# The gate product and the residual sum of each routed block, moved from VectorE to GpSimd

## The reference, cut to what matters

```
h = layernorm(x) * (1 + ca) + sa
x = x + ga * mixer(h)                        # the part that the change touches
h = layernorm(x) * (1 + cb) + sb
scores = softmax(h @ gate_w.T); the best 2 of 8 experts per token
x = x + gb * (sum over the 2 experts + silu(h @ sw1.T) * (h @ sw2.T) @ sw3.T)
```

## Time and profile before

| | us |
|---|---|
| median of 3 runs | 2100.26 |
| lowest and highest | 2099.86, 2103.84 |
| the profiled execution | 2101.66 |
| its span in the trace | 2099.8 |

### The profile page before, as it was taken

The page is one execution under the profiler, slowest core; times in us unless marked ns, Lnnn a source line. Parts: engine busy times, 40 slices in busy tenths (PEclk is TensorE's granted clock), DMA queues, the critical chain, the costliest instruction groups (busy, mean ns, idle before and its releaser), DMA issues.

```text
span 2099.8 us, 25086 instructions
## 1 busy us (share of the span) xinstructions
PE 1815.3 (86%) x6766; PEld 825.8 (39%) x6766; DVE 1938.2 (92%) x1839; ACT 1559.2 (74%) x3223; POOL 1791.2 (85%) x607
## 2 busy tenths in 40 slices
PE   7898898979797888889897979797877599999997
PEld 3323332323232323233332323242312156668996
DVE  7988999999999999999999999999999977746776
ACT  5886879797978888776779797979876444446664
POOL 5689999999999999999999999999999834324555
PEclk9989898989898988989898989898967699999999
DMA  7745454453535362635454453535361483224554
GB/s 264 241 122 139 117 136 112 112 131 108 129 105 130 95 160 67 157 90 138 109 137 113 118 127 110 127 109 121 85 150 43 148 326 118 89 101 81 95 97 74
DMA packets 140219, 264.24 MB, mean 126 GB/s; under 512 B 21376, under 2 KB 43904, under 8 KB 138928
## 3 DMA queue, kind: packets, MB, share of 16 engines
q1 hardware_dynamic: 125488, 240.90, 42.6%
q0 software_dynamic: 13296, 17.80, 4.9%
q10 hardware_dynamic: 1296, 3.93, 0.5%
HBM read 193.36 MB, written 70.26 MB: 126 GB/s over the span
## 4 chain that ended last, share of the span: by engine, by line
ACT 27%; DVE 25%; PE 24%; issue 15%; POOL 6%; DMA 1%; DVEq 0%; ACTq 0%; POOLq 0%; SPq 0%
DVE hst L1656 17%; ACT psum L1282 11%; DVE dbu L1635 6%; PE psum L2260 5%; POOL hst L963 4%; ACT dbu L1314 3%; PE psum L2347 3%; PE psum L2356 3%; PE psum L2367 3%; PE psum L2273 3%; PE psum L2102 2%; POOL dbu L951 2%; ACT L1211 2%; PE psum L2034 1%; ACT sp_tmp L1251 1%
## 5 line engine op out<-in xcount | busy, mean ns | idle before, releaser
L963 POOL TENSOR_TENSOR hst<-hst,c_rep 128x2048 f32<-128x2048 f32 x254 | 1145.0, 4534 | 5.8 <-DVE hst L1656 5.8
L1656 DVE TENSOR_TENSOR_SCAN hst<-psum,state,dbu 128x1024 f32<-128x1024 f32 x384 | 879.0, 2329 | 0.3 <-PE psum L2102 0.2
L1282 ACT ACTIVATE psum<-dt_rep,neg_a 128x512 f32<-128x512 f32 (+1 forms) x1024 | 660.2, 676 | 151.1 <-DVE hst L1656 148.5
L1635 DVE TENSOR_TENSOR dbu<-psum,b_rep 128x2048 f32<-128x2048 f32 x176 | 398.2, 2262 | 3.3 <-PE psum L2087 3.3
L951 POOL TENSOR_TENSOR dbu<-dtu_rep,b_rep 128x2048 f32<-128x2048 f32 x80 | 363.7, 4546 | 16.5 <-DVE hst L1656 11.5
L2102 PE MATMUL psum<-hst,same 128*32 128x512 f32 x2048 | 275.4, 686 | 53.6 <-POOL hst L963 47.4
L2087 PE MATMUL psum<-dt,same 32*128 32x512 f32 x352 | 217.0, 699 | 119.7 <-DVE dbu L1635 105.2
L1656 DVE TENSOR_TENSOR_SCAN hst<-psum,dbu 128x1024 f32<-128x1024 f32 x128 | 286.6, 2272 | 12.7 <-ACT psum L1282 8.8
L2034 PE MATMUL psum<-xp,taps 128*128 128x512 f32 x512 | 236.8, 606 | 9.5 <-ACT sp_tmp L1248 9.5
L1072 POOL DMA_INDIRECT out_x<-h,target_u x71 | 111.5, 1571 | 120.0 <-DVE h L1952 51.8
L2102 PEld LDWEIGHTS psum<-hst,same 128*32 128x32 f32 x2048 | 66.5, 124 | 271.1 <-issue 166.9
(11 more groups left out here) (194 smaller groups left out, 2566.8 us busy)
## 6 DMA issues: line engine op xcount, KB each, us to landing
dt_rep<-dt_scratch SPq DMA_DIRECT2D x256, 256.0 KB, 4.7
dtu_rep<-dtu_scratch SPq DMA_DIRECT2D x320, 64.0 KB, 1.9
taps<-taps_scratch SPq DMA_DIRECT2D x64, 256.0 KB, 4.4
b_rep<-bc_scratch SPq DMA_DIRECT2D x64, 256.0 KB, 5.1
c_rep<-bc_scratch SPq DMA_DIRECT2D x64, 256.0 KB, 7.7
dt_scratch<-dt SPq DMA_DIRECT2D x48, 256.0 KB, 6.1
h<-slot_scratch SPq DMA_DIRECT2D x71, 129.5 KB, 2.5
sp_tmp<-t_scratch SPq DMA_DIRECT2D x16, 512.0 KB, 6.9
```

What stands on the lines that cost most here:

```text
L963: nc.gpsimd.tensor_tensor(h, h, c_rep[q % 2][:], ALU.mult).then_inc(prod_done, 1)
L1282: nc.scalar.activation(psum[:, PS_A + i, kept], dt_rep[:, G % 2, j, kept], ACT.Exp, scale=neg_a[:, q % 2, u, i:i + 1]).then_inc(exp_done, 1)
L1635: nc.vector.tensor_tensor(dbu[:, U % DBU, :, :], psum[:, PS_U:PS_U + 1, :].broadcast_to((P, NG, TB)), b_rep[U // UNITS % 2][:], ALU.mult). ...
L1656: nc.vector.tensor_tensor_scan(both(hst[:, U % RING, groups, :]), both(psum[:, PS_A + 2 * pair:PS_A + 2 * pair + 2, :]), both(dbu[:, U % D ...
```

## The change

Both instructions of `add_mixed` move from VectorE to GpSimd, with the same operands. On GpSimd the blocks 0 and 1 come straight behind the last `weigh` and in front of the first two `norm_power`; block `p + 1` comes at the start of iteration `p`, in front of `scatter(p - 1, 0)`, and so straight behind `scatter(p - 2, 1)`. SyncE, ScalarE and TensorE keep their programs. The semaphore `f_x1` is now raised by GpSimd.

```diff
+            def add_mixed(p):
+                n, half = TAKEN[p], p % 2
+                pool.wait_ge(f_in[half], 32 * (p // 2) + 32)
+                block_x1 = x1[:, rows_of(n), :]
+                gates = fmod[:, n // SEG, 0:1, :].broadcast_to((P, NT, DM))
+                nc.gpsimd.tensor_tensor(tin[:, half], tin[:, half], gates, ALU.mult).then_inc(f_x1, 1)
+                pool.wait_ge(f_x1, 2 * p + 1)
+                nc.gpsimd.tensor_tensor(block_x1, block_x1, tin[:, half], ALU.add).then_inc(f_x1, 1)
...
+            pool.wait_ge(f_gate_loaded, 32)
+            for p in range(2):
+                add_mixed(p)
             for p in range(2):
                 norm_power(p)
...
             for p in range(NBLK):
+                if 0 < p < NBLK - 1:
+                    add_mixed(p + 1)
                 if p > 0:
                     scatter(p - 1, 0)
...
-            def add_mixed(p):
...
             dve.wait_ge(f_gate_loaded, 32)
-            add_mixed(0)
             norm_statistics(0)
...
-            add_mixed(1)
             norm_statistics(1)
...
             for p in range(1, NBLK - 1):
                 shared(0, p - 1)
-                add_mixed(p + 1)
                 shift_logits(p)
```

## The result

| | before | after |
|---|---|---|
| median | 2100.97 (4 runs, 2099.86 to 2103.84) | 2123.23 (4 runs, 2121.62 to 2128.80) |
| the profiled execution | 2101.66 | 2122.43 |
| its span | 2099.8 | 2120.5 |

The kernel before has one run more here than in the table ahead of the prediction. The change makes the kernel 1.06% slower: ratio 1.0106, 95% interval 1.0087 to 1.0126, or +22.3 us. The forecast was +8.3 us, and the range ended at 2114.5. The direction and both places of the loss were as forecast. The size was not.

The account below looks back on a forecast made before the run. TensorE was taken to bound the routing period, so freeing VectorE pays almost nothing. The terms 2.4 - 0.5 + 1.2 + 5.2 = +8.3 us gave a median of 2108.6 us, range 2101.5 to 2114.5.

Parts of the forecast that it names:

- block 2's sum gone from beside the first scatter DMA: First routing period: scatter(0, 0)'s first DMA shortens from 1.47 to 0.96 us, on the path, -0.5 us.
- GpSimd's two-input 128x1024: Length of each moved instruction on GpSimd, from a line through sizes 512 and 2048: 2.36 us.
- collision A: Mixer's end: GpSimd's block 0 product runs between VectorE's two last mixer products, delaying sum_chunk: +2.4 us (0 to +4.7).
- collision B: End of rank_experts: GpSimd's mixing holds short VectorE instructions, delaying behind: +1.2 us in the first period, +5.2 over four.
- other moves, SyncE's loads, the power: Routing stage: SyncE's loads, scatter(p - 1, 0) and norm_power have time in hand, no cost.
- What bounds the kernel: Routing stage: TensorE is busy the whole 23.0 us period, VectorE has over 5 us idle.
- The port: SBUF port shared by VectorE and GpSimd, held for a whole instruction: costs where both run at once.
- The scatter's 0.5 us: First period: scatter(0, 0)'s first DMA at 1.47 us beside VectorE's sum, 0.96 undisturbed, so -0.5 us.
- Rival 3: It compounds: GpSimd first at both L1840, late block 2 data, or late ScalarE scaling; 2113 to 2120, chance 0.12.
- Rivals 1 and 2: Rival 1: only collision A counts, 2102.2, chance 0.17; rival 2: VectorE keeps the port when it matters, about 2099.5, chance 0.13.

Follow-up runs that it names:

- x7: Changed kernel plus expert-stage count clamp, blocks 0 and 1 mixed on VectorE, blocks 2 to 7 on GpSimd but behind place_tokens: 2105.32 us, ratio 1.0014.
- x8: Changed kernel plus expert-stage count clamp, with 7 dummy matmuls on TensorE ahead of count_places each period (15 in the first): 2123.98 us, ratio 1.0089.
- x5: Kernel before plus expert-stage count clamp, with 9, 12, 15 and 12 idle bn_stats on VectorE before the last ranking instruction of four iterations: 2114.88 us, ratio 1.0049.
- x9: Changed kernel with only the count GpSimd waits for in each expert tile bounded from below by 0: 2124.62 us, ratio 1.0094.
- x1: Changed kernel plus expert-stage count clamp, with blocks 0 and 1 mixed by VectorE again, blocks 2 to 7 by GpSimd: 2121.28 us, ratio 1.0095.
- x4: Changed kernel plus expert-stage count clamp, with 14 dummy matmuls on TensorE ahead of count_places (30 in the first period): 2130.04 us, ratio 1.0142.
- x3: Changed kernel plus expert-stage count clamp, with GpSimd's mixing of block p + 1 held until VectorE's place_tokens of block p - 1: 2108.77 us, ratio 1.0046.
- x6: Changed kernel plus expert-stage count clamp, with only the products on GpSimd and the sums back on VectorE: 2111.76 us, ratio 1.0035.

## Why the prediction was wrong

| step of the prediction | said | measured |
|---|---|---|
| block 2's sum gone from beside the first scatter DMA | -0.5 | 1.24 us for 1.47: -0.2 |
| GpSimd's two-input 128x1024 | 2.36 | 2.35 |
| collision A | +2.4 (0 to 4.7) | +4.2 at the first logits |
| first period, collision B | +1.2 (up to 3.6) | wait 3.52, period +5.2 |
| four periods, collision B | +1.3 each | waits 1.65, 1.64, 1.60, 1.65; periods +3.61, +3.60, +1.86, +3.61 |
| TensorE's clock behind the waits | not in the sum | about +1.75 in three of the four, some 1.6 in the first |
| other moves, SyncE's loads, the power | 0 | no wait for the loads; L1713 waits 1.42 for the power where L1708 waited 0.95, once |

*What bounds the kernel* was right: TensorE bounds the period and freed VectorE time pays nothing (x7). *The port* was right in kind: VectorE was held at both places that it named.

**The step that failed is the price of TensorE's wait.** The prediction took a wait of 1.3 us as 1.3 us. The wait itself was 1.65, but three of the four periods lost 3.6. The missing part is the clock at 1.2 GHz behind it. x8 shows it from one side (no gap, no slow stretch, the periods 1.7 us shorter where it had fallen), x5 from the other (a gap made by VectorE alone brings it back). In the first period x8's filler saves 27.93 - 26.28 = 1.65 us. With the three others that is about 7 us of the 22, and half of the 14 that the forecast missed. The other half is the sizes of the holds, below. The trace of before could have warned, though it shows no wait in a steady period: the earlier trace rows has the granted clock at 0.83 in the first stretch, where TensorE is busy for 26.5 of 36 us, and 1.00 in the two where it is busy for 19.6 of 21 us and for all of 23. The prediction quoted these rows and priced nothing from the column.

**Collision A was mis-sized by its order of turns.** The prediction let VectorE go first and said +4.7 if GpSimd goes first both times. It did: 10.35 for 5.91 us. That was a choice between two stated ends, made on one row. The row at 12.88 in the earlier trace rows on which I chose the middle had an idle GpSimd arriving behind VectorE, and at the mixer's end GpSimd came straight from another instruction. That makes some 2 us of the miss.

**Collision B started one instruction earlier.** The forecast had L1750, L1751 and L1752 of before held and the instructions in front safe. Instead L1745 of before was held, though by its record it began 0.43 us ahead of the product and lasts 0.42 by itself. Two holds came to 4.23 us instead of 3.7, so 0.35 us more wait in each of four periods, 1.4 us. In the first period both L1755 and L1757 were held (L1750 and L1752 of before). The prediction had L1750 already past, L1751 slipping in and one hold, +1.2 us, and the wait was 3.52, 2.3 more and near its own upper end of 3.6.

**The scatter's 0.5 us was misread.** The first DMA of a scatter was compared with the last of another one (0.96). In the changed kernel, where VectorE's sum is gone, the first takes 1.24, and the earlier trace rows has one of 1.27, so some 0.2 us could go and not 0.5. That they lie on the path is argued and not shown.

Together: 8.3 + 1.8 (A) + 0.3 (scatter) + 2.3 (first period) + 1.4 (four periods) + 1.3 (some 0.26 around each of five waits) + 6.9 (clock, 1.65 + 3 x 1.75) = 22.3, against the routing stage's 22.1. Without the clock it would be 15.4, so the sizes alone would have carried the time past the end of the range.

Rival 3, that it compounds, had GpSimd first at both L1840 and a time of 2113 to 2120. It was right on that place and still lacked the clock. Rivals 1 and 2 are out.

**What stays open.** Whether a wait of 1.6 us costs the clock differs from one to the next: behind 1.6 us or so it fell at three of four places in the changed kernel and at two of the same four in x9, x5 has two waits of 1.81 us of which one was followed by it, and x1 has a wait of 3.15 us with 3.60 behind it. Nor is the price fixed: in x9's first period the clock was down for twice as long, and the period is 3.5 us longer than with the filler in x8. Against that, no slow stretch stands behind `count_places` in any of the twelve periods of x4 and x8 that had a filler in place of the wait. No run here tells what decides. The Trainium skill ("TensorE: Matmul & The Clock Gate", section "Part 1: The HAM clock gate (the "warmup" mystery)") has the clock follow TensorE's recent activity, looked at in a rhythm of its own that no kernel starts. That the places change between two executions with equal waits fits, but it was not tested. Nor was it measured from when on a VectorE instruction is held ahead of GpSimd's recorded start.

## What to carry to other kernels

Before moving an elementwise instruction to an idle GpSimd, ask what VectorE executes at that moment, and lay the GpSimd work where VectorE waits, reduces or reads PSUM: the same instructions cost 18 us at one place of the period and nothing where they began 6.4 us later, in x3 (its product waits that long for the places and starts at 1748.00). Where TensorE bounds a stage, sum the holds on the chain that feeds it and subtract the slack. Price what is left at more than itself, since a wait of 1.6 us on a TensorE that was busy all the time cost 1.9 to 3.6 us in the steady periods here.

## What the runs showed of the hardware

- GpSimd kept its turn against a waiting VectorE from one instruction to the next when it had nothing left to wait for between them (4.64 us for two products, in x6). At its gap of 0.08 us, where it waited for itself, one VectorE instruction got in, and the next GpSimd one went ahead of VectorE's second.
- A VectorE instruction of 0.42 us whose record starts 0.42 or 0.43 us before GpSimd's was still held for the whole product, in the changed kernel (3.08) and in x6 (3.07).
- A one-input `tensor_scalar` of 128x32 was held like the others (2.78 us for 0.18), and a reduction of 128x256 was not (0.42), nor was a product of 128x512 with one input in PSUM (0.69, in x3).
- TensorE's clock was at 1.2 GHz behind three of four waits of 1.6 us in the changed kernel, while TensorE had been and was again busy all the time. Each fall cost some 1.7 us there. It was at 1.2 GHz for nearly 7 us behind a wait of 3.69 us in x9 and behind one of 2.03 us in x1.
